# An RWKV block beside a top-1 mixture of experts on one core: the channel mix's value product in quarters in the next step, the last sums on TensorE, accumulating stores, and a sixth buffer for expert weights

## The chip, the cores and the metric

The kernel runs on one core of a Trainium2 chip. The metric is the device time of one execution in microseconds (us), lower is better. One execution was also taken by the hardware profiler, and the rows below come from that one.

## The reference

The input x has 32 sequences of 256 tokens with 128 channels, 8192 tokens in all. Everything is float32.

```
xn  = layernorm(x)
# branch 1: RWKV
z = layernorm(xn, ln1);  d = z - shift(z)
k, v, r = three mixes of (z, shift z), each times a 128x128 matrix
rwkv = sigmoid(r) * wkv(k, v)          # a scan over the 256 tokens
x2 = xn + rwkv @ att_ow.T
h = layernorm(x2, ln2), mixed with shift(h)
kk = relu(xk @ f_kw.T) ** 2            # 512 wide
s = x2 + sigmoid(xr @ f_rw.T) * (kk @ f_vw.T)
# branch 2: shared expert, and one of 8 routed experts per token
y = swiglu_shared(xn) + swiglu_e(xn * score)      # e = argmax of xn @ gate_w.T
# result
out = x + s * silu(y)
```

## The kernel before, in words

The tokens are cut into 16 chunks of 512. A prologue loads x, normalises it into XN, transposes it into XT and computes the routing. Then come the steps. Step i works on three chunks at once: the scan of chunk i, the channel mix of chunk i-1, and the mixes and keys of chunk i+1. Every engine has its own hand-written list for a step (the functions `step` at lines 513, 712, 865 and 1121), and between its entries stand eight places, `fill(i, 0)` to `fill(i, 7)`, into which a static plan (lines 41 to 68) puts other work: "S" and "D" are the shared expert (28 items of 14 chunks in steps 0 to 5, those of the last two chunks in step 16), "E" is one tile of 128 tokens of a routed expert (71 tiles and two slots on either side, eight to a step, steps 6 to 14), and "Z" is a part of the final combination (from step 15 on). An engine executes its list strictly in order.

Of step i, for later reference, the order on TensorE is: `attention_out` (L408, writes bank FB), `z1_transpose` (L378), places 0 to 4 with `z2_transpose` (L414) after place 4, places 5 and 6, `ffn_receptance` (L420), place 7, then `ffn_key` 0 and 1 (L431), `key_value`, `ffn_key` 2 and 3, `receptance` of the next chunk (L399, writes FA, waits for the third relu), and the whole `ffn_value` (L440, 32 matmuls, one accumulation in bank BO). VectorE begins with `make_x2` (L1044), has the scans, `time_mixes` (L985) and `channel_mixes` (L1058, L1061) in the middle, then the two squares (L1069), `running_max`, `differences` (L999, L1000, L1004), and last `make_s` (L1074, L1077), which waits for `ffn_value`. ScalarE ends a step with a table load (L735), relu 0 and 1 (L650), a square, Ln and Exp, relu 2 and 3, a square, two Exps and a second table load (L749). GpSimd does the small statistics of x2 (L823 to L829), one difference (L815), the indirect DMAs (rows scattered by expert L841, expert results scattered back L849) and the product `make_rw` (L837), for which `attention_out` of the next step waits.

An expert slot n does on TensorE: gate and up of tile n (L486, 8 matmuls), the transpose of tile n+2 (L493) and down of tile n-2 (L500), the latter two into one bank, BX. ScalarE copies BX out (L689), then takes the silu of the gate (L692), then scales the rows of tile n+4 (L675). VectorE multiplies by up (L1093). The SyncE queue loads the tile's expert weights (384 KB, L298) into one of NEW = 5 buffers, when the slot that used the buffer has finished, and then the rows of tile n+4 (L292), for which it waits until GpSimd's scatter of tile n-6 has landed: both stand in one queue, alternately.

The final combination ("Z", chunk c) waits for all routed results, which SyncE reads back (L322). VectorE adds them to the shared part in XT (L1105), ScalarE takes the silu (L699), VectorE multiplies by s (L1100) and adds the x that SyncE has loaded again (L1110, L317), and SyncE stores (L326). Six chunks stand in step 15, seven in step 16, the rest in step 17.

## Time and profile before

| | us |
|---|---|
| median of 3 runs | 581.18 (580.44 to 582.52) |
| the profiled execution, its own time | 577.9 |
| its span, first to last instruction | 576.1 |
| prologue and step 0 | 101.2 |
| steps 1 to 5 (shared expert in the places) | 137.7 |
| steps 6 to 13 (routed experts in the places) | 233.2 |
| step 14 | 26.9 |
| step 15 | 34.5 |
| step 16 and the end | 42.6 |

A step is taken to begin where VectorE starts `make_x2` (L1044), which happened at 101.2, 129.3, 157.6, 184.7, 211.8, 238.9, 271.4, 299.9, 329.1, 357.6, 386.4, 414.9, 443.4, 472.1, 499.0 and 533.5 us. In the rows, PE is TensorE, PEld its weight loads, DVE VectorE, ACT ScalarE, POOL GpSimd and SP SyncE; a name in brackets is what ended an engine's idle time.

### The profile page before, as it was taken

The page shows a single profiled execution, that of the slowest core. Times are in us where ns is not written, and L with a number is a line of the kernel's source. Part 1 is how long each engine was busy: PE and PEld are TensorE (multiplying, and loading weights), DVE is VectorE, ACT ScalarE, POOL GpSimd, SP SyncE. Part 2 cuts the span into 40 slices and gives each one's busy share as a digit, 9 for nine tenths or more (in the row PEclk, how much of TensorE's full clock was granted, in tenths as well). Part 3 has the DMA queues.
Part 4 walks back from the last instruction along what each step waited for, and adds up shares of the span by engine and source line. Part 5 has one row for each costly group of instructions (what it writes and reads, how often), then busy time and mean ns, then how long its engine had stood idle before and what let it go on. Part 6 is the DMA issues. An engine that isn't in the chain of part 4 may idle for free. (4 is left out here: it accounts for less than half of the span.)

```text
span 576.1 us, 8950 instructions
## 1 busy us (share of the span) xinstructions
PE 464.0 (81%) x2623; PEld 345.9 (60%) x2623; DVE 425.2 (74%) x836; ACT 345.6 (60%) x707; POOL 264.7 (46%) x317
## 2 busy tenths in 40 slices
PE   0989777797979797889898989898989897637661
PEld 0989244564646464787777777777777776425341
DVE  3553795879697977695969596969696968783766
ACT  3776423665646566676776677677777676536441
POOL 6664003657575858461818181818181828210100
PEclk9999988999899999999999999999999999957986
DMA  6329404010000001262727282727272825245482
GB/s 200 110 75 257 96 0 155 22 36 26 33 25 33 31 27 38 62 186 73 221 71 211 84 222 73 209 85 220 73 225 71 226 66 167 73 136 158 128 236 73
DMA packets 68864, 64.97 MB, mean 113 GB/s; under 512 B 5952, under 2 KB 57025, under 8 KB 68816
## 3 DMA queue, kind: packets, MB, share of 16 engines
q1 hardware_dynamic: 63344, 54.31, 34.5%
q0 software_dynamic: 4320, 8.53, 4.2%
q10 hardware_dynamic: 1152, 1.56, 0.8%
q8 instruction: 21, 0.34, 0.2%
q14 instruction: 27, 0.22, 0.1%
HBM read 46.86 MB, written 17.97 MB: 113 GB/s over the span
## 5 line engine op out<-in xcount | busy, mean ns | idle before, releaser
L849 POOL DMA_INDIRECT routed_out<-xh,xs x71 | 91.3, 1286 | 30.2 <-ACT xh L689 16.1
L486 PE MATMUL bank_ring<-xh,ew 128*128 128x128 f32 x568 | 78.6, 281 | 19.9 <-DMA ew<-ex_w 9.3
L486 PEld LDWEIGHTS bank_ring<-xh,ew 128*128 128x128 f32 x568 | 68.8, 191 | 26.9 <-ACT xh L689 15.2
L841 POOL DMA_INDIRECT tokens_by_expert<-xn,pos x64 | 67.2, 1051 | 37.0 <-issue 18.5
L1069 DVE TENSOR_TENSOR kk<-rk 128x512 f32<-128x512 f32 x32 | 26.3, 822 | 54.3 <-ACT rk L650 54.3
L689 ACT ACTIVATE xh<-bank_ring 128x256 f32<-128x256 f32 (+1 forms) x75 | 27.8, 371 | 63.4 <-PE bank_ring L500 62.3
L440 PEld LDWEIGHTS bank_out<-fvw,kk 128*128 128x128 f32 x512 | 60.9, 195 | 8.2 <-issue 8.2
L440 PE MATMUL bank_out<-fvw,kk 128*128 128x128 f32 x512 | 60.8, 278 | 0.0
L823 POOL TENSOR_SCALAR x_sm<-x_mv 128x4 f32<-128x4 f32 x16 | 3.8, 235 | 111.8 <-DVE x_mv L1051 111.8
L470 PE MATMUL bank_ring<-xt,sup 128*128 128x512 f32 x64 | 34.9, 628 | 17.5 <-DVE hs L1085 10.6
L837 POOL TENSOR_TENSOR rw<-den_num,lq 128x512 f32<-128x512 f32 x16 | 20.3, 1269 | 53.8 <-issue 46.5
L500 PE MATMUL bank_ring<-ew,hx 128*128 128x128 f32 x284 | 43.5, 276 | 0.7 <-DVE hx L1093 0.7
L449 PEld LDWEIGHTS bank_ring<-sdn,hs 128*128 128x128 f32 x256 | 31.6, 196 | 15.8 <-DVE hs L1085 12.0
L500 PEld LDWEIGHTS bank_ring<-ew,hx 128*128 128x128 f32 x284 | 38.1, 194 | 1.0 <-ACT xh L689 0.9
L1093 DVE TENSOR_TENSOR hx<-px,bank_ring 128x256 f32<-128x256 f32 x71 | 29.0, 408 | 13.1 <-ACT px L692 12.9
L431 PE MATMUL bank_fa<-xk,fkw 128*128 128x512 f32 x64 | 36.4, 653 | 2.3 <-ACT rk L650 2.3
L449 PE MATMUL bank_ring<-sdn,hs 128*128 128x128 f32 x256 | 32.3, 280 | 6.9 <-DVE hs L1085 6.9
L464 PE MATMUL bank_ring<-xt,sup 128*128 128x512 f32 x64 | 34.9, 628 | 2.3 <-ACT tg L668 2.3
L431 PE MATMUL bank_fb<-xk,fkw 128*128 128x512 f32 x64 | 34.3, 617 | 3.0 <-ACT tf L644 3.0
L1085 DVE TENSOR_TENSOR hs<-tg,bank_ring 128x512 f32<-128x512 f32 x32 | 21.7, 679 | 17.5 <-ACT tg L668 11.8
L470 PEld LDWEIGHTS bank_ring<-xt,sup 128*128 128x128 f32 x64 | 11.4, 193 | 38.7 <-DVE hs L1085 18.0
L572 ACT ACTIVATE xn<-xi,nb,rs 128x128 f32<-128x128 f32 x64 | 26.3, 482 | 12.1 <-POOL nb L801 11.9
(139 smaller groups left out, 1124.0 us busy)
## 6 DMA issues: line engine op xcount, KB each, us to landing
ew<-ex_w SPq DMA_DIRECT2D x71, 384.0 KB, 4.0
xi<-x SPq DMA_DIRECT2D x32, 256.0 KB, 3.7
tokens_by_expert<-pad_row SPq DMA_DIRECT2D x1, 4686.0 KB, 21.2
xs<-tokens_by_expert SPq DMA_DIRECT2D x71, 66.0 KB, 3.6
ew<-routed_out SPq DMA_DIRECT2D x16, 256.0 KB, 3.3
out<-xn SPq DMA_DIRECT2D x16, 256.0 KB, 3.2
routed_out<-xh,xs POOLq DMA_INDIRECT x71, 4.1
tokens_by_expert<-xn,pos POOLq DMA_INDIRECT x64, 2.3
```

The source lines that it names most:

```text
L431: nc.tensor.matmul((FA, FB)[q % 2][:, :], part(FKW, q, P), XK2[:, :], start=True, stop=True)\
L440: last = nc.tensor.matmul(part(BO, j, CH), KK[:, q * CHUNK + j * P:q * CHUNK + (j + 1) * P], part(FVW, q, CH), start=(q + j == 0), stop=(q ...
L449: last = nc.tensor.matmul(part(b, j, CH), h[:, q * CHUNK + j * P:q * CHUNK + (j + 1) * P], part(SDN, q, CH), start=(q == 0), stop=(q == EQ ...
L464: nc.tensor.matmul(ring(5 * m + 3 * q)[:, :], part(SUP, q, P), part(XT, m, CHUNK), start=True, stop=True)\
L470: nc.tensor.matmul(ring(5 * m + 3 * q + 1)[:, :], part(SUP, EQ + q, P), part(XT, m, CHUNK), start=True, stop=True).then_inc(s_su, 1)
L486: last = nc.tensor.matmul(part(GU[n % 2], q, P), part(w, q, P), xt[:, 0:P], start=True, stop=True)
L500: last = nc.tensor.matmul(BX[:, P:P + CH], part(h, q, P), part(w, 2 * EQ + q, CH), start=(q == 0), stop=(q == EQ - 1))
L572: last = nc.scalar.activation(xn_tile(t), part(XI[c % 4], j, P), ACT.Identity, bias=NB[:, t:t + 1], scale=RS[:, t:t + 1])
L689: nc.scalar.activation(XH[n % NXH][:, a:b], BX[:, a:b], ACT.Copy).then_inc(s_xh, 1)
L841: nc.gpsimd.indirect_dma_start(xs_dram, bass.IndirectOffsetOnAxis(ap=POS[:, t:t + 1], axis=0), XN[:, t * XROW:(t + 1) * XROW], None).then_ ...
L849: nc.gpsimd.indirect_dma_start(routed_dram, bass.IndirectOffsetOnAxis(ap=XS[(n - 2) % NXS][:, CH:CH + 1].bitcast(i32), axis=0), XH[n % NXH ...
L1093: nc.vector.tensor_tensor(HX[n % NHX][:, :], PX[n % 2][:, :], GU[n % 2][:, EF:2 * EF], ALU.mult)\
```

## The change

- Expert weights get six buffers. In a slot, ScalarE takes the silu before the copy out of BX.
- `ffn_value` of chunk i-2 is done in step i, a quarter (8 matmuls) after each of places 0 to 3, and `make_s` of chunk i-2 on VectorE after place 3. Only the last chunk's is done at the end of step 16. X2 gets two buffers for this, so that `make_x2` no longer waits for the `make_s` before it. `attention_out` stands before place 0 and the transposes a place later or earlier; `ffn_key` 0 and 1 stand before place 7; ScalarE's relu 0 and 1 move in front of the table load, its Ln and Exp in front of the square; VectorE's `time_mixes` go behind `channel_mixes`.
- The shared expert is finished in steps 0 to 6: five items in each of steps 1 to 4, four in step 5, none in step 16.
- In the final combination TensorE adds routed and shared part as two products with the identity into a bank (`final_sum`), from which ScalarE takes the silu. For chunks 0 to 11 nothing is added on VectorE: x is copied to the output in DRAM early by one DMA of 3 MB, and GpSimd stores s times silu with an accumulating DMA. Chunks 12 to 15 are added on VectorE and stored by SyncE as before.

The diff, cut to its core:

```diff
-NXS, NEW, NXH, NHX, AHEAD = 12, 5, 8, 3, 4
+NXS, NEW, NXH, NHX, AHEAD = 12, 6, 8, 3, 4
...
-EARLY, LATE = 14, 16
 E_STEP = 6
+ADDED = 12
 
 
 def plan():
 
 
     steps = [[[] for _ in range(8)] for _ in range(CHUNKS + 2)]
-    shared = [("S", m, q) for m in range(EARLY) for q in range(2)] + [("D", EARLY - 1, 0)]
+    shared = [("S", m, q) for m in range(CHUNKS) for q in range(2)] + [("D", CHUNKS - 1)]
     for k in range(8):
         steps[0][k].append(shared.pop(0))
     for i in range(1, E_STEP):
-        for k in (0, 2, 4, 6):
+        for k in (0, 1, 3, 5, 7) if i < E_STEP - 1 else (0, 2, 4, 5):
             steps[i][k].append(shared.pop(0))
     steps[E_STEP][0] += shared
...
-    late = [("S", m, q) for m in range(EARLY, LATE) for q in range(2)] + [("D", LATE - 1, 0)]
-    for k, item in zip((0, 1, 2, 3, 4), late):
-        steps[CHUNKS][k].append(item)
...
-        X2, Z2 = sb("x2", CHUNK), sb("z2", CHUNK)
+        X2, Z2 = [sb(f"x2_{u}", CHUNK) for u in range(2)], sb("z2", CHUNK)
...
+            sp.dma_start(out[0:ADDED * CHUNK, :], x[0:ADDED * CHUNK, :]).then_inc(s_pre, 16)
...
-            def load_final_x(c):
-                if c >= 4:
-                    sp.wait_ge(s_fo, c - 3)
-                else:
-                    sp.wait_ge(s_xn, CHUNKS)
-                sp.dma_start(tiles(XI[c % 4][:, :]), rows(x, c)).then_inc(s_fx[c % 4], 16)
-
             def load_final_routed(c):
                 if c >= 4:
                     sp.wait_ge(s_fy, c - 3)
                 sp.dma_start(tiles(RR[c % 4]), rows(routed_dram, c)).then_inc(s_fr_in[c % 4], 16)
 
             def store(c):
-                sp.wait_ge(s_fo, c + 1)
-                sp.dma_start(rows(out, c), xn(c)).then_inc(s_out[c % 4], 16)
-
-            for c in range(4):
-                load_final_x(c)
+                sp.wait_ge(s_fo, c - ADDED + 1)
+                sp.dma_start(rows(out, c), xn(c)).then_inc(s_last, 16)
+
+            sp.wait_ge(s_xn, CHUNKS)
+            for c in range(ADDED, CHUNKS):
+                sp.dma_start(tiles(XI[c % 4][:, :]), rows(x, c)).then_inc(s_fx[c % 4], 16)
             for u in range(NXH):
                 sp.wait_ge(s_yo[u], 16 * sum(1 for m in range(2, XTILES + 2) if m % NXH == u))
-            for c in range(4):
+            for c in range(CHUNKS):
                 load_final_routed(c)
-            for c in range(CHUNKS):
-                if c + 4 < CHUNKS:
-                    load_final_routed(c + 4)
-                if c > 0:
-                    store(c - 1)
-                    if c + 3 < CHUNKS:
-                        load_final_x(c + 3)
-            store(CHUNKS - 1)
+            for c in range(ADDED, CHUNKS):
+                store(c)
             for u in range(4):
-                sp.wait_ge(s_out[u], 16 * (CHUNKS // 4))
+                sp.wait_ge(s_out[u], 16 * (ADDED // 4))
+            sp.wait_ge(s_last, 16 * (CHUNKS - ADDED))
...
-            def ffn_value(c):
-                if c > 0:
+            def ffn_value(c, q):
+                if q == 0 and c > 0:
                     pe.wait_ge(s_u, c)
-                for q in range(FQ):
-                    pe.wait_ge((s_kk, s_kd)[q % 2], 2 * c + 1 + q // 2)
-                    for j in range(TPC):
-                        last = nc.tensor.matmul(part(BO, j, CH), KK[:, q * CHUNK + j * P:q * CHUNK + (j + 1) * P],
-                                                part(FVW, q, CH), start=(q + j == 0), stop=(q + j == FQ + TPC - 2))
-                last.then_inc(s_kv, 1)
+                pe.wait_ge((s_kk, s_kd)[q % 2], 2 * c + 1 + q // 2)
+                for j in range(TPC):
+                    last = nc.tensor.matmul(part(BO, j, CH), KK[:, q * CHUNK + j * P:q * CHUNK + (j + 1) * P],
+                                            part(FVW, q, CH), start=(q + j == 0), stop=(q + j == FQ + TPC - 2))
+                if q == FQ - 1:
+                    last.then_inc(s_kv, 1)
...
-                    if m == EARLY:
-                        pe.wait_ge(s_hx, XTILES)
-                        pe.wait_ge(s_xh, XTILES + 4)
...
+            def final_sum(c):
+                if c < CHUNKS:
+                    b = RING[c % 3]
+                    pe.wait_ge(s_fr_in[c % 4], 16 * (c // 4 + 1))
+                    if c >= 3:
+                        pe.wait_ge(s_fw, c - 2)
+                    elif c == 0:
+                        pe.wait_ge(s_hx, XTILES)
+                        pe.wait_ge(s_xh, XTILES + 4)
+                    nc.tensor.matmul(b[:, :], ident, RR[c % 4], start=True, stop=False)
+                    nc.tensor.matmul(b[:, :], ident, part(XT, c, CHUNK), start=False, stop=True).then_inc(s_fy, 1)
...
-                C, P1 = 0 < i <= CHUNKS, i + 1 < CHUNKS
+                C, P1, V = 0 < i <= CHUNKS, i + 1 < CHUNKS, 1 < i <= CHUNKS
                 if C:
                     attention_out(i - 1)
+                fill(i, 0)
                 if P1:
                     z1_transpose(i + 1)
-                fill(i, 0)
+                if V:
+                    ffn_value(i - 2, 0)
                 fill(i, 1)
+                if V:
+                    ffn_value(i - 2, 1)
                 fill(i, 2)
                 if i == 0:
                     routing_prefix()
+                if V:
+                    ffn_value(i - 2, 2)
                 fill(i, 3)
+                if C:
+                    z2_transpose(i - 1)
+                if V:
+                    ffn_value(i - 2, 3)
                 fill(i, 4)
-                if C:
-                    z2_transpose(i - 1)
                 fill(i, 5)
+                if C:
+                    ffn_receptance(i - 1)
                 fill(i, 6)
-                if C:
-                    ffn_receptance(i - 1)
-                fill(i, 7)
                 if C:
                     ffn_key(i - 1, 0)
                     ffn_key(i - 1, 1)
+                fill(i, 7)
                 if P1:
                     key_value(i + 1)
                 if C:
@@ -540,8 +547,9 @@
                     ffn_key(i - 1, 3)
                 if P1:
                     receptance(i + 1)
-                if C:
-                    ffn_value(i - 1)
+                if i == CHUNKS:
+                    for q in range(FQ):
+                        ffn_value(i - 1, q)
...
-            for i in range(CHUNKS + 1):
+            for i in range(CHUNKS + 2):
...
+                if 0 <= n < XTILES:
+                    act.wait_ge(s_gu, n + 1)
+                    nc.scalar.activation(PX[n % 2][:, :], GU[n % 2][:, 0:EF], ACT.Silu).then_inc(s_px, 1)
...
-                if 0 <= n < XTILES:
-                    act.wait_ge(s_gu, n + 1)
-                    nc.scalar.activation(PX[n % 2][:, :], GU[n % 2][:, 0:EF], ACT.Silu).then_inc(s_px, 1)
...
-                    nc.scalar.activation(part(XT, c, CHUNK), part(XT, c, CHUNK), ACT.Silu).then_inc(s_fw, 1)
+                    nc.scalar.activation(part(XT, c, CHUNK), RING[c % 3][:, :], ACT.Silu).then_inc(s_fw, 1)
...
                 fill(i, 2)
-                fill(i, 3)
                 if T:
                     receptance(i)
+                fill(i, 3)
+                if C:
+                    make_h2(i - 1)
                 fill(i, 4)
-                if C:
-                    make_h2(i - 1)
                 fill(i, 5)
+                if C:
+                    ffn_tanh(i - 1)
                 fill(i, 6)
                 if C:
-                    ffn_tanh(i - 1)
+                    ffn_relu(i - 1, 0)
                 fill(i, 7)
+                if C:
+                    ffn_relu(i - 1, 1)
                 if T:
                     nc.scalar.preload_act_table_set("natural_log_exp_and_others")
-                if C:
-                    ffn_relu(i - 1, 0)
-                    ffn_relu(i - 1, 1)
+                    inverse_of_den(i)
+                if C:
                     ffn_square(i - 1, 0)
-                if T:
-                    inverse_of_den(i)
-                if C:
                     ffn_relu(i - 1, 2)
...
+            def final_store(c):
+                if 0 < c <= ADDED:
+                    if c == 1:
+                        pool.wait_ge(s_pre, 16)
+                    pool.wait_ge(s_fv, c)
+                    settle(pool)
+                    nc.gpsimd.dma_start(rows(out, c - 1), xn(c - 1), accum_op=ALU.add).then_inc(s_out[(c - 1) % 4], 16)
...
-                    dve.wait_ge(s_s, c)
                     dve.wait_ge(s_z2, TPC * c)
-                nc.vector.tensor_tensor(tiles(X2[:, :]), tiles(FB[:, :]), xn(c), ALU.add).then_inc(s_x2, 1)
+                if c > 1:
+                    dve.wait_ge(s_s, c - 1)
+                x2 = X2[c % 2]
+                nc.vector.tensor_tensor(tiles(x2[:, :]), tiles(FB[:, :]), xn(c), ALU.add).then_inc(s_x2, 1)
...
-                if c < CHUNKS:
-                    dve.wait_ge(s_fr_in[c % 4], 16 * (c // 4 + 1))
-                    dve.wait_ge(s_sh, c + 1)
-                    nc.vector.tensor_tensor(part(XT, c, CHUNK), RR[c % 4], part(XT, c, CHUNK), ALU.add).then_inc(s_fy, 1)
-                if c > 0:
+                if c > ADDED:
                     u = (c - 1) % 4
                     dve.wait_ge(s_fv, c)
-                    dve.wait_ge(s_fx[u], 16 * ((c - 1) // 4 + 1))
+                    dve.wait_ge(s_fx[u], 16)
...
                 fill(i, 3)
+                if i == 0:
+                    routing_rows()
+                if V:
+                    make_s(i - 2)
+                if C:
+                    channel_mixes(i - 1)
+                fill(i, 4)
                 if P1:
                     time_mixes(i + 1)
...
-                if C:
-                    channel_mixes(i - 1)
                 fill(i, 5)
```

## Rows read from the trace of the kernel before

**Rows 1.** Busy time by stretch: step 4, steps 6 to 13, step 15, and the rest.
The columns are: stretch, length, busy time and instructions of PE, PEld, DVE, ACT, POOL, granted clock, DMA share, GB/s.

```profile
184.70:211.80 27.10, 23.83 (x119) 15.09 (x118) 22.69 (x36) 16.07 (x27) 17.80 (x18) 1.00 0.09 31
...
238.90:472.10 233.20, 207.54 (x1417) 169.12 (x1417) 180.15 (x321) 163.23 (x370) 113.73 (x111) 1.00 0.51 144
...
...
499.00:533.50 34.50, 15.98 (x62) 10.64 (x63) 23.10 (x40) 13.97 (x23) 6.01 (x5) 0.65 0.43 123
533.50:576.10 42.60, 21.46 (x99) 13.05 (x97) 29.20 (x52) 15.44 (x28) 2.57 (x4) 0.85 0.51 148
```

**Rows 2.** Timeline of TensorE in step 9: start, length, instruction.

```profile
357.23 1.06 PE L486 MATMUL bank_ring<-xh,ew 128*128 128x128 f32 x8
...
358.68 1.06 PE L486 MATMUL bank_ring<-xh,ew 128*128 128x128 f32 x8
...
371.55 1.06 PE L420 MATMUL bank_fb<-att,xr 128*128 128x128 f32 x8
...
374.26 1.02 PE L431 MATMUL bank_fa<-xk,fkw 128*128 128x512 f32 x2
...
380.22 1.10 PE L399 MATMUL bank_fa<-xr,att 128*128 128x512 f32 x2 [0.65 <-ACT rk L650]
381.16 3.73 PE L440 MATMUL bank_out<-fvw,kk 128*128 128x128 f32 x32
384.73 1.06 PE L408 MATMUL bank_fb<-att,rw 128*128 128x128 f32 x8
```

**Rows 3.** Waits of TensorE in steps 7 to 12: total us, times, longest.

```profile
PE bank_ring L486 <- DVE hx L1093: 6.3, 12, 0.6
PE bank_ring L486 <- DMA ew<-ex_w: 6.2, 10, 0.7
PE bank_fa L399 <- ACT rk L650: 3.9, 6, 0.7
```

**Rows 4.** Timeline of VectorE in step 9.

```profile
357.61 0.69 DVE L1044 TENSOR_TENSOR x<-bank_fb,xn 128x512 f32<-128x512 f32 x1
...
370.52 0.75 DVE L1061 SCALAR_TENSOR_TENSOR xr<-d,vectors,h 128x512 f32<-128x512 f32 x1
...
380.60 0.95 DVE L1069 TENSOR_TENSOR kk<-rk 128x512 f32<-128x512 f32 x1 [0.90 <-ACT rk L650]
...
382.73 0.73 DVE L1004 SCALAR_TENSOR_TENSOR dd<-pp,vectors,bank_k 128x512 f32<-128x512 f32 x1
...
386.43 0.69 DVE L1044 TENSOR_TENSOR x<-bank_fb,xn 128x512 f32<-128x512 f32 x1
```

**Rows 5.** Timeline of ScalarE in step 9.

```profile
375.43 1.28 ACT L735 ACT_TABLE_LOAD   x1
...
379.98 0.59 ACT L650 ACTIVATE rk<-bank_fb 128x512 f32<-128x512 f32 x1
```

**Rows 6.** Groups of instructions by line and form in steps 7 to 12.
The columns are: count, busy us in total, mean ns of one, idle time before.

```profile
L849 POOL DMA_INDIRECT routed_out<-xh,xs x48 | 61.6, 1283 | 20.4 <-ACT xh L689 11.3 <-issue 9.2
...
L1093 DVE TENSOR_TENSOR hx<-px,bank_ring 128x256 f32<-128x256 f32 x48 | 19.5, 407 | 7.1 <-ACT px L692 7.1
...
L826 POOL TENSOR_TENSOR x_sm<-x_sm,minus_half 128x4 f32<-128x4 f32 x6 | 6.2, 1041 | 0.0
```

**Rows 7.** Timeline of TensorE in step 15.

```profile
508.04 1.11 PE L414 MATMUL bank_fb<-consts,z 128*128 128x128 f32 x4 [9.71 <-ACT z L629]
```

**Rows 8.** Timeline of GpSimd in step 15.

```profile
502.80 1.97 POOL L826 TENSOR_TENSOR x_sm<-x_sm,minus_half 128x4 f32<-128x4 f32 x1
```

**Rows 9.** Timeline of VectorE at the end.

```profile
572.56 0.69 DVE L1110 TENSOR_TENSOR xn<-xn,xi 128x512 f32<-128x512 f32 x1
```

**Rows 10.** DMA issues: engine, count, KB each, median us from issue to landing.

```profile
tokens_by_expert<-pad_row SPq DMA_DIRECT2D x1, 4686.0 KB, 21.2
...
out<-xn SPq DMA_DIRECT2D x16, 256.0 KB, 3.2
```

**Rows 11.** Waits of the SyncE queue, 240 to 480 us: total us, times, longest.

```profile
SPq L292 <- DMA routed_out<-xh,xs: 17.3, 15, 2.3
```

36 lines of the change are left out of this document (20 added, 16 removed).

## Prediction

> **What bounds the kernel now.** I read the busy times by stretch first, then TensorE's timeline and waits in one expert step, then the other engines' timelines there, and last the two closing steps. Eight steps with routed experts take 233.2 us; in them TensorE is busy 207.5 us, VectorE 180.2, at full clock [rows 1]. Step 6 holds about 4 us of start-up, so an ordinary step lasts (233.2 - 3.9) / 8 = 28.7 us. TensorE's work in it: a slot takes 358.68 - 357.23 = 1.45 us, eight take 11.6; the whole value product takes 384.73 - 381.16 = 3.57 [rows 2]; key, key-value and the other wide products come in pairs, six of them between 374.26 and 380.22 less the wait of 0.65, so 0.88 each and 7 in a step, 6.2 us; four groups of narrow ones add 2.7. Together 24.1 us: 4.6 us a step is idle. Rows 3 name most of it: over six steps 6.3 us for VectorE's product in a slot, 6.2 us for the expert weights, 3.9 us for a relu before the next receptance.
>
> The order explains the rest. VectorE works without a gap from `make_x2` (357.61) past the mixes (370.52) [rows 4]; slots wait for it there. After the last slot (374.26, where the keys begin) it is the other way round: table load 375.43, fourth relu 379.98 + 0.59 [rows 5], receptance 380.22, value product, `make_s`, and only then the next `make_x2` at 386.43. So a step is 16.65 us from `make_x2` to the end of the last slot and 12.17 from there to the next `make_x2`.
>
> The last two steps are another regime: 34.5 and 42.6 us with TensorE busy 16.0 and 21.5 us, its clock at 0.65 and 0.85 [rows 1]. VectorE has the most to do and ScalarE waits for its sums.
>
> **Expert steps (6 to 13).** The value product leaves the serial end of a step, and its quarters (0.89 us) fall between slots where TensorE waits for VectorE. The new cycle, followed along its tightest chain:
> - From `make_x2` to the receptance product: 371.55 - 357.61 = 13.94 [rows 2, 4]. Out of it go three time mixes (of the kind of L1061, issued 0.67 apart: 2.0) and one slot product (0.33 of 0.41 net [rows 6]); in comes `make_s`, two operations of 0.69 [rows 4]: 13.0.
> - Receptance 0.89, slot 1.45, keys 0 and 1 1.75, slot 1.45: 5.5.
> - Last slot to relu 1: now 375.43 - 374.26 = 1.17, less the silu (0.27) that moves in front of the copy: 0.9.
> - Relu 1 to the end of relu 3: 380.57 - 375.43 = 5.14 [rows 5] less the 0.49 of relu 0, which is earlier: 4.65. TensorE's receptance of the next chunk waits for relu 2 there, its `attention_out` for relu 3, so some 1.7 us of idle stay.
> - Square 3 and `differences`, 380.60 to 383.46 [rows 4]: 2.9, then `make_x2`. `make_s` is gone from here.
>
> Sum 27.0 us, against 28.7: 1.7 less in each of 8 steps, **-14 us**. The quarters lie beside it, as does `make_z1`. The bound from above is 28.7 (nothing gained), the one from below TensorE's own 24.1 plus the 1.7: 25.8, -23 us. The sixth buffer removes the weights' wait, since a load is issued one slot (1.45 us and more) earlier and the longest wait is 0.7 [rows 3]; as VectorE's chain sets the cycle then, it adds nothing of its own.
>
> **Steps 1 to 5.** They take 137.7 us now. Ten shared products, 3.5 us of pairs for each two items, move in from step 16: four items (7.0 us) and two downs (3.6); step 1 loses its value part (-3.6). Step 4 has 23.8 us busy of 27.1 [rows 1], its real content being 12.5 + 10.6 = 23.1. With five items the content is 24.2 to 26.1; adding the 1.7 us at relu 2 and, in steps with three downs, a wait of about 1.4 us for `make_s` and the mixes, I get 28.5 and 26.1 in turn, 26 for steps 1 and 5: 135. I take **-2**, between -7 (only content counts) and +6. The copy of 3 MB into the output stands beside them: the fill of 4.7 MB took 21.2 us [rows 10], so about 14; nobody waits for it until step 15, and it delays the weights by nothing, as they are issued before it. Its cover is this quiet stretch, DMA share 0.09 [rows 1]. Step 14 has fewer slots: **-1**.
>
> **Step 15.** z2 is transposed 508.04 - 499.0 = 9.0 us after `make_x2` [rows 7, 1]; I keep that, though three sums on TensorE fit in front. Then a quarter 0.9, `make_s` 1.4 and half the mixes 1.6, with latencies 13.3; receptance 0.9; a sum is two wide products by the identity, four instructions, 1.75; sum, keys, sum: 5.2, so 19.4; silu 0.8; relu 1 to 3 4.65; `attention_out` 0.9: 25.8 us, say 26, **-8**. The full clock is assumed: the 0.65 came where TensorE had stood idle for 9.71 us [rows 1, 7]. At 1.2 GHz the eight products on the chain would add 3 us.
>
> **Step 16 and the end.** TensorE content from `attention_out` on: seven sums 12.2, two value products 7.1, transpose and receptance 1.3, keys 3.5, three more sums 5.2: 29.3. The last silu 0.8, two VectorE operations 1.4, and then what follows the last L1110 now, 576.1 - 573.25 = 2.85 [rows 9]: 34.4. **-8**. Five shared items and their waits are gone from here, and L1105 of every chunk with L1110 of twelve.
>
> GpSimd gets twelve stores of 512 rows. The nearest rows are an indirect DMA of 128 rows, 1.28 us on GpSimd [rows 6], and a SyncE store of the same 256 KB, 3.2 us to landing [rows 10]. So a store costs GpSimd between 0 (below nothing is excluded, it is added work) and 4 x 1.28 = 5.1 us. I take 3, since it is a direct store like that one, and not an indirect one. From the first possible one, 10 us into step 15, to the end there are 60 - 10 - 4 = 46 us, so up to 3.9 us each nothing waits for them, except `make_rw` and the statistics of x2 that stand behind them in GpSimd's list.
>
> GpSimd's power operation took 1.97 us in step 15 against 1.04 elsewhere [rows 8, 6], just when VectorE ran its scans. The Trainium skill (SBUF — State Buffer, "Who interferes with whom") says that a VectorE instruction with two SBUF inputs holds off a GpSimd instruction that reads SBUF; the row agrees. By it step 16, where a silu product now stands at place 0, would be about 1 us longer than summed.
>
> **Sum.** -14 - 2 - 1 - 8 - 8 = -33 us: 577.9 - 33 = 544.9 for the profiled execution. That one is 3.3 us under the median 581.2, which I carry over: **548**. A measurement of this kernel can tell about 0.3% from no change.
>
> **Rivals.**
> 1. The expert steps gain nothing (12%): every engine's order changes, and a wait of a slot takes the value's place. For it: VectorE and ScalarE both run in strict order, and 12 waits for hx [rows 3]. Against: the serial `make_s` is gone. 562.
> 2. The sixth buffer does not do what it says (8%): a weight load stands behind a rows load that waits for a scatter, 17.3 us in 15 waits [rows 11]. Then 6.2 / 6 = 1.0 us a step stays: 556.
> 3. Stores hold GpSimd 5.1 us each (12%): 12 x (5.1 - 3.9) = +15: 563.
> 4. Slower (5%): accumulating stores take so long that they set the end. They decide from 3.9 us each on, and eat the whole gain from 3.9 + 33 / 12 = 6.7 us; at 8 us the time is 548 + 49 = 597. Twice the landing of a plain store is 6.4 [rows 10]. The Trainium skill (Collectives: The Full Stack, "The bandwidth ceiling") says that an add in a DMA needs two source reads and so runs at about half the rate. No row here has such a DMA. Against the rival: 256 KB in 4 us are 66 GB/s, and steps 6 to 13 moved 144 [rows 1].
> 5. Better (10%): slots flow freely and a step takes 25.8: 548 - 9, and with the shared steps at their content 534.
>
> My forecast has 50%, and 3% is left for no change at all (something unseen costs 33 us). The range takes in cases 1, 2, 3 and most of 5: 534 to 565. Faster 0.92, same 0.03, slower 0.05.
>
> **What would show it.** In the profile after, an expert step should be 27 us from one `make_x2` to the next, no wait for `ew` left, the receptance's wait for relu grown from 0.65 to about 1.7, and idle before `make_s` near nothing. Steps 1 to 5 should stay at 135 +- 5. Step 15 should fall to 26 with a clock near 1, the rest to 34, ending on a SyncE store of chunk 15. Wrong would be: GpSimd at or near full in steps 15 and 16, the last landing an accumulating one, or TensorE's gaps in slots simply moved to after the quarters.

## The result, and the profile after

The changed kernel took 564.85 us (median of 4, 564.21 to 568.7) where the kernel before took 581.85 (580.44 to 583.52) beside it: a ratio of 0.972 [0.967, 0.977]. It is faster by 17 us, where 33 were forecast; the profiled execution took 565.1 us and not 544.9. Measured again later, on four more occasions and each time on another chip, the same unaltered kernel gave 547.0, 545.8, 547.1 and 555.9 us, so the first thing to learn here is which part of a time belongs to a program. The steps, by the starts of `make_x2`:

| us | before | forecast | after, first trace | after, second (e5) |
|---|---|---|---|---|
| prologue and step 0 | 101.2 | 101.2 | 97.0 | 97.3 |
| steps 1 to 5 | 137.7 | 135 | 153.9 | 136.2 |
| steps 6 to 13 | 233.2 | 219 | 222.2 | 220.6 |
| step 14 | 26.9 | 26 | 24.8 | 24.8 |
| step 15 | 34.5 | 26 | 29.3 | 29.2 |
| step 16 and the end | 42.6 | 34.4 | 36.1 | 36.0 |

The first trace by stretch (columns as in [rows 1]), step 4, steps 6 to 13, an ordinary expert step, and the last two:

```profile
187.80:224.50 36.70, 29.34 (x126) 17.70 (x125) 22.03 (x37) 16.18 (x28) 17.20 (x18) 0.88 0.07 23
250.90:472.90 222.00, 200.10 (x1413) 168.18 (x1412) 177.38 (x321) 168.40 (x371) 111.87 (x111) 0.99 0.51 152
283.90:310.90 27.00, 24.48 (x176) 20.53 (x176) 22.18 (x41) 20.73 (x46) 14.03 (x14) 1.00 0.52 156
497.90:527.20 29.30, 22.00 (x77) 12.78 (x76) 16.41 (x30) 15.87 (x26) 12.06 (x10) 0.89 0.62 108
527.20:563.30 36.10, 31.18 (x124) 17.90 (x123) 17.95 (x33) 12.19 (x22) 11.36 (x11) 0.93 0.69 124
```

An ordinary expert step is 27.0 us, seven times in a row: the forecast's figure. Its waits on TensorE, steps 7 to 12 together, against [rows 3]:

```profile
PE bank_fa L387 <- ACT rk L658: 10.9, 6, 1.8
PE bank_fb L408 <- DVE xr L1082: 4.3, 6, 0.7
```

No wait for expert weights and none for hx (VectorE's product in a slot) is left; the wait for relu grew from 0.65 to 1.8 us a step. The rows of step 9 on TensorE, VectorE and ScalarE carry the chain:

```profile
350.88 1.16 PE L408 MATMUL bank_fb<-att,xr 128*128 128x128 f32 x8 [0.72 <-DVE xr L1082]
...
353.49 1.02 PE L419 MATMUL bank_fa<-xk,fkw 128*128 128x512 f32 x2
...
356.66 1.02 PE L371 MATMUL bank_k<-xk,att 128*128 128x512 f32 x2
...
362.07 1.10 PE L387 MATMUL bank_fa<-xr,att 128*128 128x512 f32 x2 [1.81 <-ACT rk L658]
```

```profile
362.44 0.69 DVE L1090 TENSOR_TENSOR kk<-rk 128x512 f32<-128x512 f32 x1 [2.45 <-ACT rk L658]
...
364.97 0.68 DVE L1064 TENSOR_TENSOR x<-bank_fb,xn 128x512 f32<-128x512 f32 x1
```

```profile
357.43 0.59 ACT L658 ACTIVATE rk<-bank_fb 128x512 f32<-128x512 f32 x1
...
361.82 0.59 ACT L658 ACTIVATE rk<-bank_fb 128x512 f32<-128x512 f32 x1
```

`make_x2` of this step starts at 337.94. So: 12.9 us to the receptance (forecast 13.0), 5.8 to the end of the last slot at 356.66 (5.5), 0.8 to relu 1 (0.9), 5.0 to the end of relu 3 (4.65), 2.6 to the next `make_x2` (2.9).

**Where the missing time is.** Steps 1 to 5 took 18.9 us more than forecast. In step 4, TensorE stands still for 6 us in front of key 1, waiting for the tanh:

```profile
201.88 1.95 PE L437 MATMUL bank_ring<-sdn,hs 128*128 128x128 f32 x16
204.65 1.16 PE L408 MATMUL bank_fb<-att,xr 128*128 128x128 f32 x8 [0.82 <-issue]
205.65 1.02 PE L419 MATMUL bank_fa<-xk,fkw 128*128 128x512 f32 x2
212.74 2.07 PE L419 MATMUL bank_fb<-xk,fkw 128*128 128x512 f32 x2 [6.06 <-ACT tf L652]
```

and ScalarE's tanh (L652) stands behind the copy of a down product (L670), which waited 8 us:

```profile
211.60 0.60 ACT L670 ACTIVATE xt<-bank_ring 128x512 f32<-128x512 f32 x1 [8.00 <-remote]
212.09 0.59 ACT L652 ACTIVATE tf<-bank_fb 128x512 f32<-128x512 f32 x1
212.57 0.61 ACT L658 ACTIVATE rk<-bank_fa 128x512 f32<-128x512 f32 x1
```

```profile
ACT xt L670 <- remote: 17.2, 3, 8.0
```

TensorE's clock falls to half about then, for 6.8 us each time (at 121.6, 183.1 and 210.4 us; the wide product at 212.74 takes 2.07 us, otherwise 1.02).

In the expert steps, too, the products of one slot report up to 1.6 us late in this trace, at no cost: the steps take 27.0 us.

### The profile page after: what moved, and what is told of

Its sections match the earlier page's. It is cut to its first block and busy times, and to the rows that moved or that the text cites. A ratio compares the mean times of both kernels' runs of the same rounds, so it can differ in the third digit from the quotient of the medians.

```text
span 563.3 us, 9051 instructions
## 1 busy us (share of the span) xinstructions
PE 482.9 (86%) x2687; PEld 359.8 (64%) x2687; DVE 401.3 (71%) x808; ACT 353.4 (63%) x707; POOL 277.4 (49%) x329
## 5 line engine op out<-in xcount | busy, mean ns | idle before, releaser
L849 POOL DMA_INDIRECT tokens_by_expert<-xn,pos x64 | 68.8, 1074 | 35.1 <-issue 18.5
L471 PE MATMUL bank_ring<-xh,ew 128*128 128x128 f32 x568 | 76.7, 279 | 0.0
L471 PEld LDWEIGHTS bank_ring<-xh,ew 128*128 128x128 f32 x568 | 70.7, 194 | 4.5 <-issue 3.8
L1090 DVE TENSOR_TENSOR kk<-rk 128x512 f32<-128x512 f32 x32 | 24.2, 755 | 63.1 <-ACT rk L658 63.1
L427 PE MATMUL bank_out<-fvw,kk 128*128 128x128 f32 x512 | 67.5, 278 | 0.0
L427 PEld LDWEIGHTS bank_out<-fvw,kk 128*128 128x128 f32 x512 | 63.5, 195 | 3.9 <-issue 3.9
L692 ACT ACTIVATE px<-bank_ring 128x256 f32<-128x256 f32 x71 | 27.1, 381 | 34.9 <-PE bank_ring L471 31.0
L845 POOL TENSOR_TENSOR rw<-den_num,lq 128x512 f32<-128x512 f32 x16 | 20.2, 1262 | 44.4 <-issue 39.4
L387 PE MATMUL bank_fa<-xr,att 128*128 128x512 f32 x32 | 19.3, 687 | 24.0 <-ACT rk L658 23.1
L670 ACT ACTIVATE xt<-bank_ring 128x512 f32<-128x512 f32 x16 | 9.6, 597 | 43.0 <-PE bank_ring L437 21.7
```

Source lines behind the costliest of these rows:

```text
L427: last = nc.tensor.matmul(part(BO, j, CH), KK[:, q * CHUNK + j * P:q * CHUNK + (j + 1) * P], part(FVW, q, CH), start=(q + j == 0), stop=(q ...
L471: last = nc.tensor.matmul(part(GU[n % 2], q, P), part(w, q, P), xt[:, 0:P], start=True, stop=True)
L692: nc.scalar.activation(PX[n % 2][:, :], GU[n % 2][:, 0:EF], ACT.Silu).then_inc(s_px, 1)
L849: nc.gpsimd.indirect_dma_start(xs_dram, bass.IndirectOffsetOnAxis(ap=POS[:, t:t + 1], axis=0), XN[:, t * XROW:(t + 1) * XROW], None).then_ ...
```

## The experiments

**First group: what makes the signals late?** All four vary the changed kernel.

e1: in the shared places TensorE waits for its own signals, so that it never runs on past one.

```diff
                 if q == 0 and m > 0:
                     shared_down(m - 1)
+                if m >= 4:
+                    pe.wait_ge(s_su, 2 * m + q + 1)
+                    if q == 0:
+                        pe.wait_ge(s_sd, m)
```

> The changed kernel with one thing added: in steps 1 to 5 TensorE waits, after each shared item, for the semaphores that its own last products of that item raise. Theory A (TensorE's signals come late because a long stretch of products without a pause builds up a backlog, and that is what made steps 1, 3 and 4 of the changed kernel 32, 32 and 37 us long): the backlog cannot grow, no signal is late by over 0.5 us, steps 1 to 5 take 138 to 143 us in place of 153.9, the kernel about 552 us. Theory B (GpSimd's bursts of twelve scatters hold the signals up until the last has landed): the signals stay late, TensorE merely waits for them itself, steps 1 to 5 take 154 us or more, the kernel 565 or more. Theory C (five items are too much content for such a step): 25 short pauses of 0.1 to 0.2 us are added, 157 us, 568.

e2: four shared items a step instead of five; the rest stands at the start of step 6.

```diff
-        for k in (0, 1, 3, 5, 7) if i < E_STEP - 1 else (0, 2, 4, 5):
+        for k in (0, 1, 3, 5):
```

> The changed kernel with four shared items in each of steps 1 to 5 (places 0, 1, 3, 5) and the last four items with the last down in a burst at the head of step 6, before the expert slots. Theory C (content): steps 1 to 5 fall to 130 to 135 us, step 6 grows by the burst, 11 us of products, from 33 to about 44: 557. Theory A (backlog of signals): with 1.7 to 3.5 us less to do in a step TensorE pauses more often, fewer late signals, 135 to 140 us, kernel 558 to 563. Theory B (scatters): the signals stay late, steps 1 to 5 at 148 or more, kernel 570.

e3: GpSimd's scatters of rows by expert are left out, and with them the routed part's data (the closing reads take x in its place).

```diff
-                for _, t in zip(range(count), sending):
-                    scatter_rows(t)
+                pass
```

> The changed kernel without GpSimd's 64 indirect scatters of rows (and without the waits for them); the final combination reads x in place of the routed results, so the routed part is left out, with all its instructions still executed on rows that belong to no token. Theory B: no late signals of TensorE in steps 1 to 5, which take 135 to 140 us; kernel about 550. Theories A and C: the signals are late where they were, steps 1 to 5 take 150 to 154 us, kernel 561 to 565.

e4: the sixth buffer alone is undone.

```diff
-NXS, NEW, NXH, NHX, AHEAD = 12, 6, 8, 3, 4
+NXS, NEW, NXH, NHX, AHEAD = 12, 5, 8, 3, 4
```

> The changed kernel with five buffers for expert weights in place of six, all else the same. The forecast said that VectorE's chain sets the cycle of an expert step and that the sixth buffer adds nothing of its own: then steps 7 to 13 stay at 27.0 us and the kernel at 565. The rival: the weights' wait of the kernel before comes back, 1.0 us in each of eight steps, 28 us a step and 573.

Measured beside a kernel before of 579.6 us: e1 550.8 (ratio 0.948 [0.945, 0.951]), e2 554.1 (0.955 [0.952, 0.958]), e3 546.4 (0.943 [0.939, 0.946]), e4 547.3 (0.943 [0.941, 0.945]). Not one signal is late in any of the four traces, and steps 1 to 5 take 131 to 139 us. e4 touches nothing that bears on those steps, so edits could not be the reason; the same kernel had to be run again. It also follows that e1 to e3 decide nothing about what makes signals late, since there were none to remove: that e1's 550.8 us lie near the 552 of its theory A means nothing, and beside e4 its waits cost 3.5 us. Of itself e4 says that the sixth buffer brings nothing: expert steps are 27.0 us with five as with six, and with five, too, TensorE has no wait for expert weights left. e2 says that five items a step are right: its steps 1 to 5 are 5 us shorter than e4's, but step 6 takes 42.5 us instead of 31.4.

**Second group: the same kernel again, and three terms of the sum.** e5 has no edit.

> The changed kernel itself, not a letter altered, beside the kernel before. In its first trace some of TensorE's completion signals came 0.8 to 7.8 us late and steps 1 to 5 took 153.9 us, while four kernels close to it, measured later beside one another, had none and took 136 to 139. Theory A, the lateness belongs to this program (its long stretches of TensorE without a wait together with its exact timing): it comes again, about 565 us, steps 1 to 5 near 154, late signals in the trace. Theory B, it belongs to the chip or the circumstances of the first runs: no late signal, steps 1 to 5 at 136 to 139, and about 547 to 549 us, level with the five-buffer variant (547.3).

It took 547.0 us (545.95 to 550.08) beside 578.4: 0.947 [0.944, 0.949]. No signal is late. The same three rows in its step 4:

```profile
194.97 0.60 ACT L670 ACTIVATE xt<-bank_ring 128x512 f32<-128x512 f32 x1 [2.04 <-PE bank_ring L437]
195.86 0.60 ACT L652 ACTIVATE tf<-bank_fb 128x512 f32<-128x512 f32 x1 [0.29 <-PE bank_fb L408]
196.72 0.60 ACT L658 ACTIVATE rk<-bank_fa 128x512 f32<-128x512 f32 x1 [0.26 <-PE bank_fa L419]
```

The copy starts 0.04 us after the down product's recorded end. Laid side by side, the two traces have the same instructions in the same order, and TensorE's starts in the first one drift away from those in the second in a few places only: +4.8 us over steps 1 and 2, +4.1 at the stall of step 3, +9.0 in step 4, each made of stalls and the half clock behind them, and 1.3 of half clock in step 6. They make up the 19.2 us between the two spans of 563.3 and 544.1. The second trace has uninterrupted TensorE stretches of 24.7 us, about as long as the first trace's longest (26.5), and the same bursts of scatters: neither is enough by itself to make signals late.

e6: the value product goes back, whole, to the end of the step.

```diff
-                if V:
-                    ffn_value(i - 2, 0)
...
-                if i == CHUNKS:
+                if C:
                     for q in range(FQ):
                         ffn_value(i - 1, q)
```

> The value product goes back, whole, behind the next receptance at the end of TensorE's step; make_s stays in the middle of the next step and x2 keeps two buffers. Theory A (the forecast's chain: the serial tail from relu 3 over the receptance sets the cycle): attention_out now ends 0.9 + 3.6 + 1.1 = 5.6 us after relu 3 where VectorE was ready after 2.9, so an expert step takes 27.0 + 2.7 = 29.7 us, no better than before (28.7); eight steps cost 21 us and steps 2 to 5 and 14 some 2 each: about +30 us to the changed kernel on the same chip. Theory B (only make_s mattered, TensorE's order is free): 27 to 28 us a step, under +8 us.

579.7 us (577.1 to 581.95), 32.7 more than e5 where 30 were expected, and the expert step takes 29.7 us, to the tenth what was expected. That this is 1.002 [0.9995, 1.0035] of the kernel before is a coincidence: the variant keeps `make_s` in the middle of the step, its expert steps are 1.0 us longer than those of before, and its last two steps (32.0 and 30.7 us) are still 14.4 us shorter. VectorE now waits for `attention_out`, which stands behind the 3.73 us of the product:

```profile
365.35 1.10 PE L387 MATMUL bank_fa<-xr,att 128*128 128x512 f32 x2 [1.81 <-ACT rk L650]
366.29 3.73 PE L427 MATMUL bank_out<-fvw,kk 128*128 128x128 f32 x32
369.86 1.06 PE L396 MATMUL bank_fb<-att,rw 128*128 128x128 f32 x8
```

```profile
370.95 0.69 DVE L1056 TENSOR_TENSOR x<-bank_fb,xn 128x512 f32<-128x512 f32 x1 [2.61 <-PE bank_fb L396]
```

e7: the twelve stores overwrite, and the early copy of x is gone; x is not added for chunks 0 to 11.

```diff
-xn(c - 1), accum_op=ALU.add)
+xn(c - 1))
...
-            sp.dma_start(out[0:ADDED * CHUNK, :], x[0:ADDED * CHUNK, :]).then_inc(s_pre, 16)
```

> The twelve stores of GpSimd overwrite instead of adding, and the early copy of 3 MB of x into the output is gone; x is not added for chunks 0 to 11. If accumulating stores and the copy stand beside other work, as forecast, the time is that of the changed kernel on the same chip within 1.5 us. Rival: each store takes about 3 us longer for its second read and GpSimd or the queue sets steps 15 and 16 (29.3 and 36.1 us where 26 and 34.4 were forecast): then these two steps fall by 5 us together. Second rival: the copy disturbs steps 1 to 5 and takes part in the late signals; then steps 1 to 5 fall by 2 us or more.

546.0 us against e5's 547.0, each step within 0.1 us of e5's: adding in the store and the copy cost nothing that counts. On GpSimd itself the plain stores are cheaper, 9.3 us for twelve against 15.8:

```profile
L865 POOL DMA_DIRECT2D out<-xn x12 | 9.3, 774 | 21.3 <-DVE xn L1118 19.8 <-issue 1.4
```

e8: the silu goes back behind the copy.

```diff
+                nc.scalar.activation(XH[n % NXH][:, a:b], BX[:, a:b], ACT.Copy).then_inc(s_xh, 1)
                 if 0 <= n < XTILES:
                     act.wait_ge(s_gu, n + 1)
                     nc.scalar.activation(PX[n % 2][:, :], GU[n % 2][:, 0:EF], ACT.Silu).then_inc(s_px, 1)
```

> In an expert slot ScalarE copies first and takes the silu behind it, as in the kernel before; nothing else is altered. Forecast's chain: the silu in front took 0.27 us off the way from the last slot to relu 1, so an expert step should be 27.3 us and the whole some 2.5 us longer. Rival: VectorE's product and with it the next slot get their input earlier in every slot, not only in the last: then a step grows by more, 0.5 to 1 us, 4 to 8 us in all, and TensorE waits for hx again.

550.2 us, 3.2 more than e5, with expert steps of 27.3: the forecast's 0.27 us of one silu, and no wait for hx. Step 6 pays 1.1 of it.

**Third and fourth group: why 29 and 36 us in the last two steps.** In the second trace, as in the first, the clock is 0.89 and 0.92 there:

```profile
478.70:507.90 29.20, 21.90 (x78) 12.87 (x78) 16.59 (x29) 16.10 (x26) 12.09 (x10) 0.89 0.62 110
507.90:544.10 36.20, 31.34 (x126) 18.05 (x124) 18.01 (x33) 12.19 (x22) 11.36 (x11) 0.92 0.70 124
```

The clock falls to half at 488.0 and 505.1 us, at the end of two idle stretches of TensorE, 3.62 us before z2's transposes and 3.36 before `attention_out`. e9 fills them with products that nobody reads.

```diff
+            def keep_busy(count):
+                pe.wait_ge(s_d, CHUNKS)
+                for j in range(count):
+                    nc.tensor.matmul(BK[:, :], part(FKW, 0, P), FKW[:, :], start=True, stop=True)
...
+                if i == CHUNKS:
+                    keep_busy(7)
                 if C:
                     attention_out(i - 1)
...
+                if i == CHUNKS - 1:
+                    keep_busy(8)
                 if C:
                     z2_transpose(i - 1)
```

> Fifteen wide products that nobody reads go into bank_k, which is free from step 15 on: eight in front of the transposes of z2 in step 15, where TensorE idled 3.62 us, and seven in front of attention_out in step 16 (3.36 us). In the changed kernel step 15 takes 29.2 us where 26 were forecast, with the clock at half behind either idle stretch. Theory A (the clock accounts for the excess): the granted clock stays near 1 in both steps, step 15 takes 26.5 to 27.5 us, step 16 and the end 1 us less than 36.0, the whole 2.5 to 3.5 us less. Theory B (the chain of z2, mixes and relus is longer for another reason): the clock rises and step 15 still takes 28.5 us or more; under 1 us in all.

549.7 us, 3.9 more than the changed kernel on the same chip (e11, 545.8), although the clock is 1.00 and 0.96: the eight took 6.9 us, since each of these products stands in the trace as two of 0.43 us. Step 15 takes 32.1 us, step 16 with the end 34.0. e12 has four and three in their place.

> In the run before, fifteen unread products kept the clock at 1.00 and 0.97, but each is two passes in float32, 0.86 us and not 0.43: the eight took 6.9 us where 3.6 were free, and z2's transposes came 3.3 us late. Now four (3.4 us) before the transposes and three (2.6 us) before attention_out. Theory A (the clock accounts for the excess of steps 15 and 16): the clock is at or near 1, step 15 takes 26.5 to 27.5 us in place of 29.2, step 16 with the end 34 to 35 in place of 36.0, together 3 to 4 us less than the changed kernel. Theory B (those steps are long for another reason): less than 1 us.

543.25 us (542.49 to 543.61) beside 577.6: 0.940 [0.937, 0.942], 3.8 us less than the changed kernel on the same chip (e15, 547.1). The clock is 1.00 and 0.98:

```profile
481.10:507.80 26.70, 25.41 (x91) 13.32 (x90) 16.38 (x30) 15.39 (x26) 12.09 (x10) 1.00 0.69 116
507.80:541.80 34.00, 29.10 (x124) 16.97 (x122) 17.86 (x33) 12.67 (x23) 11.34 (x11) 0.98 0.73 132
```

26.7 and 34.0 us, where 26 and 34.4 were forecast at full clock. The Trainium skill (TensorE: Matmul & The Clock Gate, Part 1) says that the clock follows how busy the array has lately been; this pair of runs agrees, with the same work of the kernel in both.

e10 gives the sums back to VectorE.

```diff
-                    nc.tensor.matmul(b[:, :], ident, RR[c % 4], start=True, stop=False)
-                    nc.tensor.matmul(b[:, :], ident, part(XT, c, CHUNK), start=False, stop=True).then_inc(s_fy, 1)
...
+                if c < CHUNKS:
+                    dve.wait_ge(s_fr_in[c % 4], 16 * (c // 4 + 1))
+                    dve.wait_ge(s_sh, c + 1)
+                    nc.vector.tensor_tensor(part(XT, c, CHUNK), RR[c % 4], part(XT, c, CHUNK), ALU.add).then_inc(s_fy, 1)
```

> The sums of routed and shared part go back to VectorE (one addition of 0.69 us a chunk), TensorE does none; quarters, stores and the rest stay as changed. TensorE is busy 31.3 of the 36.2 us from step 16 on and 17.2 us of that are sums, VectorE 18.0. Theory A (what gained in these steps is that VectorE was relieved): steps 15 and 16 with the end grow by the additions and by a TensorE clock at half, 3 to 8 us. Theory B (TensorE had become the bound of step 16, its sums are a cost): step 15 grows by 1 to 3 us, step 16 with the end falls by 4 us or more, and the whole is level or faster. Forecast by its own terms: the final part's gain is then mostly the stores' and additions' that VectorE and SyncE lost.

545.0 us beside the changed kernel's 545.8 (e11), the last two steps 63.2 us against 64.8, at a clock of 0.7. Neither theory had the steps right (28.5 and 34.7 us against 29.0 and 35.8), though B had the whole as level:

```profile
480.30:508.80 28.50, 13.61 (x54) 9.28 (x53) 19.85 (x36) 15.78 (x26) 12.65 (x10) 0.71 0.61 104
508.80:543.50 34.70, 17.76 (x84) 13.71 (x83) 23.62 (x43) 12.28 (x22) 11.73 (x11) 0.70 0.75 131
```

e16 adds unread products to it: two or one in each sum's place, four and three as in e12.

```diff
+                if c < 13:
+                    keep_busy(2 if c < 6 else 1)
```

> All sums on VectorE again, and TensorE's idle time in steps 15 and 16 filled with unread products: in each sum's place two (step 15) or one (step 16), four before z2's transposes, three before attention_out. With TensorE's sums and a full clock the last two steps took 60.7 us; with VectorE's sums and a clock of 0.70 they took 63.2. Theory A (VectorE's additions cost little, the clock did the harm): the clock near 1 and 59 to 61 us, the whole 541 to 543.5, level with that version. Theory B (VectorE's additions stand on the serial chain): 62 to 63 us although the clock is up.

546.7 us on a chip where the kernel before took 582.15, 0.938 [0.934, 0.943], level with e12's ratio; the last two steps take 59.7 us (e12: 60.7), at clocks of 1.00 and 0.87. The 541 to 543.5 us expected of the whole were missed, on a chip with late signals (below). The sums on TensorE, of which the change makes much, are worth nothing in either pair of runs: VectorE's additions cost no more, neither at a clock of 0.7 nor with the clock up.

e13 divides the sums (TensorE chunks 0 to 9, VectorE the rest), e14 adds e12's products to that.

```diff
-                if c < CHUNKS:
+                if c < SPLIT:
                     b = RING[c % 3]
```

> TensorE sums chunks 0 to 9, VectorE chunks 10 to 15. With all sums on VectorE the kernel was as fast as changed (545.0 against 545.8, last two steps 63.2 against 64.8 us), TensorE at 0.70 of its clock and 31.4 us busy, VectorE 43.5. If both engines bound by turns, the split gives step 15 of 29.0 as changed and 33.5 to 34.5 for the rest: 1.5 to 2.5 us less than the changed kernel. If the serial chain from z2 to the last relu alone sets the end, nothing changes (within 0.5 us).

> The split of the sums with the unread products of the first run of this group. If the two gains stand beside each other, 4 to 6 us less than the changed kernel, about 541 us; if both remove the same time, no better than the better of the two.

550.9 and 544.3 us: worse than the changed kernel (547.1) by 3.8, and no better than e12. In e13, TensorE waits behind its shorter list and over step 16 with the end the clock is 0.80 (39.4 us); in its second half, from 530 us on, it is 0.73.

e17 gives the kernel before the unread products, 19 in its step 15 and 4 in step 16.

```diff
+                if i == CHUNKS - 1:
+                    keep_busy(11)
                 if C:
                     z2_transpose(i - 1)
...
+                if i >= CHUNKS - 1:
+                    keep_busy(5 if i < CHUNKS else 3)
                 if C:
                     ffn_receptance(i - 1)
...
+                if i >= CHUNKS - 1:
+                    keep_busy(1)
...
+                if i == CHUNKS - 1:
+                    keep_busy(2)
```

> The kernel before, with unread products in the idle time of its last two steps: eleven before z2's transposes in step 15 (9.5 of the 9.71 us idle), five before the receptance, one before key 1, two before key 2; in step 16 three and one. Its steps 15 and 16 took 34.5 and 42.6 us at clocks of 0.65 and 0.85. By the durations at either level the products on the chain that ran at half cost 5 us in step 15 (transposes 0.5, receptance 0.9, three keys 2.6, value 1.1) and 2 in step 16. If the clock did that, the kernel gains 5 to 7 us: about 572 where it takes 578, and the part of the change that the closing steps gained by restructuring is correspondingly smaller. If the chains bind through VectorE and ScalarE, under 2 us.

580.4 us beside 582.15, 0.997 [0.995, 0.9994]. Step 15 falls from 34.5 to 31.9 at full clock, step 16 with the end rises from 42.6 to 44.2:

```profile
502.80:534.70 31.90, 26.79 (x99) 14.24 (x98) 23.33 (x39) 13.85 (x23) 6.03 (x5) 1.00 0.46 133
534.70:579.00 44.30, 25.07 (x107) 14.27 (x105) 29.28 (x53) 15.43 (x28) 2.57 (x4) 0.86 0.49 143
```

The expectation of 5 to 7 us was wrong. Step 15, where the clock did rise, gained 2.6 of the 5 us expected; in step 16 the clock stayed as it was (0.86 against 0.85) and 1.6 us were lost, and why is not shown. Together it is 1.0 us. (This chip is one with late signals, below, and the kernel before has no trace on it, so tenths mean nothing here.) Of the changed kernel's gain there, 77.1 to 65.2 us, the clock can then hardly be the larger part; the rest would be the moved work's, which no run undoes by itself.

**The changed kernel on three more chips.** e11, e15 and e18 are it, unaltered.

> The changed kernel unaltered once more. Twice now it has been measured: 564.9 us with late completion signals and 547.0 without. If the lateness belongs to particular chips, it may be met here: either 547 +- 1.5 with no stall in steps 1 to 5, or 562 to 567 with stalls of 2, 1.3 and 6.3 us at the same three places (steps 1, 3 and 4), each followed by a stretch at half clock. A time in between (550 to 560) would mean that the lateness is an accident of timing, and would differ from execution to execution.

> The changed kernel unaltered, as the base of this group and to see whether the late signals of the first trace come back. Expected 546 to 548 as in the last two, with no stall in steps 1 to 5; 562 to 567 if the lateness is a matter of the chip and this one has it.

> The changed kernel unaltered on a fifth later occasion. On the chip of the last group, where the kernel before took 582.2 us, both variants showed late completion signals of TensorE (up to 5.6 us, in steps 1 and 3 and in the expert steps); on the four chips without them the kernel before took 577.6 to 579.6 us. If the lateness belongs to certain chips and the kernel before tells which: with the kernel before at 581.5 us or more, late signals in steps 1, 3 or 4 and 550 to 567 us; with it at 580 or less, none and 545.5 to 547.5 us. A time of 547 beside 582, or of 565 beside 578, would refute it.

| chip of | kernel before, us | changed kernel, us | ratio | signals late by over 1.2 us in steps 1 to 4 |
|---|---|---|---|---|
| first result | 581.85 | 564.85 | 0.972 [0.967, 0.977] | in steps 1, 3, 4 |
| e5 | 578.4 | 547.0 | 0.947 [0.944, 0.949] | none |
| e11 | 578.8 | 545.8 | 0.944 [0.941, 0.947] | none |
| e15 | 577.6 | 547.1 | 0.947 [0.944, 0.950] | none |
| e16, e17 | 582.15 | (e16: 546.7) | (0.938) | e16 in steps 1, 3; e17 in step 1 |
| e18 | 583.3 | 555.9 (554.99 to 567.63) | 0.953 [0.947, 0.960] | in steps 1, 2, 3 |

On e18's chip the signals are late again: the signal for the copy in step 1 comes 2.9 us after its product's recorded end (in e5's step 4, 0.04).

```profile
120.78 0.60 ACT L670 ACTIVATE xt<-bank_ring 128x512 f32<-128x512 f32 x1 [4.93 <-remote]
```

## Why the prediction was right or wrong

**The step that failed: steps 1 to 5, "I take -2, between -7 and +6".** It added up content, the wait at relu 2 and a wait for `make_s` and the mixes, and had nothing for a completion signal that comes late. In the first trace the term was +16: three stalls behind late signals, up to 7.8 us, and the half clock at each. Nothing in [rows 1] or in any row of before shows a late signal, and no rival of mine had one. On chips without them the term measured -1.5 (136.2 against 137.7). Its pattern was less right than its sum: three downs stand in steps 1 and 3 only, while a sum of 135 counts 28.5 us twice in steps 2 to 4. Measured were 27.2, 26.8, 29.6, 26.3 and 26.2.

**Expert steps, -14.** Right in size and in cause, and rival 1 (no gain) fell: 27.0 us in both traces, each link within 0.4 us; e6 puts the value product back and the step is 29.7, e8 prices the silu at 0.3. The eight are 1.6 us longer than forecast in the second trace (12.6 gained), step 6 having kept a start of 4.4 us. The sixth buffer "adds nothing of its own": e4 agrees. But that it "removes the weights' wait" was wrong: with five buffers no such wait is left either, so something else in the change removed it, by elimination the new order of the step. Rival 2, that weights would still be waited for, fell with it.

**Step 14, -1:** measured -2.1.

**Step 15, -8, and step 16 with the end, -8:** measured -5.3 and -6.6. I had written "the full clock is assumed" and that at 1.2 GHz it would be 3 us more: z2's transposes came 8.8 us after `make_x2` (9.0 forecast), but the three sums in front of them did not bridge the time, and behind the 3.62 us of idle that were left the clock was at half. e12 gives 26.7 and 34.0 with it removed. The sum was right for the full clock, and the full clock was not there.

**A term that I had not looked for:** in the second trace step 0 became 3.9 us shorter. There VectorE now does the routing's arithmetic before the three time mixes and no longer after, so a product for the shared expert comes 2.3 us earlier (at 85.0), TensorE's wait of 2.41 us shrinks to 0.39, and its clock is full from 85.3 and not from 92.4. The size is not fixed: with the same step 0 the first `make_x2` stands at 98.4 us in e15, 98.7 in e18, 99.6 in e11 and even 101.8 in e13, where TensorE is at half clock from 72.7 to 79.5 and from 89.7 to 93.1. In the second trace it offsets the 4.1 us that the last two steps fell short, so that trace's agreement (its execution 545.95 us against 544.9) is in part luck: 3.9 too pessimistic at one end, 4 too optimistic at the other.

**Stores.** I took 3 us of GpSimd each, between 0 and 5.1. Twelve took 15.8 us, 1.3 each (1.6 by the row's mean, as some overlap), about the time that an indirect DMA of 128 rows takes it, so rivals 3 and 4 never came near their points of decision (3.9 and 6.7 us). A store that only writes took 0.8 (e7):

```profile
L868 POOL DMA_DIRECT2D out<-xn x12 | 15.8, 1564 | 15.7 <-DVE xn L1121 10.8 <-issue 4.8
```

```profile
out<-xn POOLq DMA_DIRECT2D x12, 256.0 KB, 6.1
```

An adding store lands after 6.1 us (7.0 in e5), SyncE's plain one after 3.2 [rows 10] and GpSimd's plain one after 3.1 (e7): about twice. The Trainium skill (Collectives: The Full Stack, "The bandwidth ceiling") says of the adding step of a collective that its two source reads halve the rate, and these rows agree. Nobody waits for it. And GpSimd's power operation took 1.97 us in step 15 of the first trace, as before, and 1.04 in step 16, so the microsecond more that I had named for step 16 by the Trainium skill (SBUF — State Buffer, "Who interferes with whom") was not there: VectorE was idle for all but 0.1 us of it. The prediction's "1.04 elsewhere" passes over step 16 of before, where it took 1.44.

**What stays open.** That lateness does not come from the program alone is shown by five measurements of one program, three of them with no late signal at all. On each chip all traces agree, late or not, but each chip was measured on one occasion only, so what belongs to the chip and what to the occasion is not told apart, nor whether the taking of the profile has a part in it. What makes the signals late is not shown; on the three chips that had it the kernel before took 581.9 to 583.3 us and on the others 577.6 to 579.6, an association and no more (the traced execution of before, 577.9, had no late signal). Nor is it shown why the stall of 8 us in step 4 appeared in the first trace only: on e18's chip step 4 took 26.9 us. The changed kernel suffers more from it (9 to 18 us, by its own medians) than the kernel before (some 4), and the traces fit a plain reason, that in steps 1 to 5 ScalarE's copy of a down product stands directly in front of the tanh or the relu that TensorE's next key waits for. That was not tried by itself.

## What to carry to other kernels

Look for the serial tail of a pipelined step, and move out of it whatever has no successor within it; its length can be added up from one timeline to a few tenths of a microsecond, and putting the piece back is the proof. Work out at which clock a stretch will run, from the idle time that the new order leaves in front of it, before taking durations at full clock; a few products without readers held it for 4 us of gain, but only where they fitted into the idle time; twice as many cost 3.9 us (e9). And before explaining a time that the sum doesn't give, run the unaltered kernel on another chip: here 546 to 565 us were one program.

## What was not expected of the hardware

- TensorE's completion signals can arrive up to 7.8 us after the recorded end of their instructions, several at once, on three of seven occasions (each on another chip) and not on the others, while the instructions themselves run on; each stall then costs a stretch at half clock on top (6.3 us of wait and 2.2 of clock in step 4).
- Unread products in the idle time gave the changed kernel 3.8 us (e12) and the kernel before 1.8 (e17), although the latter's clock had been lower (0.65 and 0.85 against 0.89 and 0.92).
- A GpSimd store of 512 rows costs that engine 1.3 us when it adds and 0.8 when it only writes (e7).
